# Bias products of the up rows dealt out among gate products, and another order of work in the tail

## What is computed

```python
x = x + s * g                      # first layer: a sparse gated product times a ternary gate
xn = _layernorm(x)
# s: a small recurrent net, width 64, depth 4
h = einsum('blv,dv->bld', xn, Win) + bin
for each of 4 layers:
    y = silu(layernorm(h, l1w, l1b))
    y = sconv(y, phazor, last_conv)            # a complex decaying scan along the sequence
    h = h + y * scl
    y = layernorm(h, l2w, l2b)
    y = silu(y @ W1.T + b1)                    # up, 64 to 256
    h = h + y @ W2.T + b2                      # down, 256 to 64
s = layernorm(h, lnl_w, lnl_b) @ Wout.T + bout # 64 to 512
g = silu(xn @ W.T + bias + low-rank experts)   # the gate, 512 to 512, the weights folded into one matrix
x = x + s * g
```

## Time and profile before

| | before |
|---|---|
| median of three executions | 606.12 us |
| lowest, highest | 604.01, 606.91 us |
| the profiled execution | 606.78 us |
| its span | 605.0 us |
| PE busy | 587.5 us (97%) |
| DVE busy | 486.8 us (80%) |
| ACT busy | 334.2 us (55%) |
| POOL busy | 170.8 us (28%) |
| mean granted clock | 0.989 |

### The profile page before, as it was taken

One profiled execution on the slowest core, in us unless ns is written; L12 is line 12 of the kernel. 1 busy time (PEld: TensorE's weight loads), 2 busy tenths in 40 slices (PEclk: granted clock), 3 DMA queues, 4 the chain that ended last, 5 costly groups with the idle time before them and its releaser, 6 DMA issues.

```text
span 605.0 us, 8900 instructions
## 1 busy us (share of the span) xinstructions
PE 587.5 (97%) x2868; PEld 455.7 (75%) x2868; DVE 486.8 (80%) x960; ACT 334.2 (55%) x567; POOL 170.8 (28%) x295
## 2 busy tenths in 40 slices
PE   7999999999999999999999999999999999999994
PEld 6887887888888888888888888887676555666542
DVE  6998899898788778788877878867889677887657
ACT  6879486266518626651852665285655344544430
POOL 2244002001000200100020010169954445454437
PEclk9999999999999999999999999999999799999998
DMA  8921000210030030003003000281220000000007
GB/s 341 333 69 45 2 0 1 71 35 2 1 104 0 0 104 0 0 0 104 0 0 104 0 0 0 72 304 54 54 55 1 0 1 1 1 1 1 1 1 277
DMA packets 18011, 32.37 MB, mean 53 GB/s; under 512 B 4054, under 2 KB 4566, under 8 KB 17980
## 3 DMA queue, kind: packets, MB, share of 16 engines
q1 hardware_dynamic: 17980, 32.00, 15.3%
HBM read 24.63 MB, written 7.36 MB: 53 GB/s over the span
## 4 chain that ended last, share of the span: by engine, by line
PE 73%; DVE 12%; POOL 4%; issue 4%; ACT 3%; DMA 2%; SPq 1%; DVEq 0%; POOLq 0%; ACTq 0%
PE ps_a L1859 15%; PE ps_b L1859 15%; PE ps_a L1892 15%; PE ps_b L2138 6%; PE ps_b L1899 3%; PE ps_a L2152 3%; DVE junk_d L1308 2%; PE ps_t L1878 2%; POOL arena L273 2%; PE ps_t L2146 2%; PE ps_a L2093 1%; PE ps_b L2100 1%; DMA arena<-in_f_w_t 1%; PE ps_a L2146 1%; ACT junk_a L977 1%
## 5 line engine op out<-in xcount | busy, mean ns | idle before, releaser
L1308 DVE TENSOR_SCALAR_CACHE_REDUCE junk_d<-k_buf,cand 128x1376 int8<-128x1376 f32 x56 | 91.9, 1640 | 0.3
L977 ACT ACTIVATE junk_a<-k_buf,cand 128x1376 int8<-128x1376 f32 x56 | 80.5, 1437 | 0.7
L956 ACT ACTIVATE s_buf<-ps_a 128x1376 f32<-128x1376 f32 x16 | 21.1, 1318 | 93.6 <-PE ps_a L1859 91.2
L1892 PE MATMUL ps_a<-wd_hi,zt_hi 128*128 128x512 f32 (+1 forms) x176 | 72.0, 409 | 0.1
L1892 PE MATMUL ps_a<-wd_hi,zt_lo 128*128 128x512 f32 (+1 forms) x176 | 69.2, 393 | 0.0
L1892 PE MATMUL ps_a<-wd_lo,zt_hi 128*128 128x512 f32 (+1 forms) x176 | 68.8, 391 | 0.0
L777 POOL TENSOR_TENSOR xres<-xres,gate 128x512 f32<-128x512 f32 x12 | 22.4, 1865 | 131.1 <-DVE gate L1434 131.1
L1859 PE MATMUL ps_a<-wg_hi,xt_hi 128*128 128x512 f32 (+1 forms) x192 | 51.9, 378 | 0.4 <-ACT s_buf L956 0.3
L1859 PE MATMUL ps_b<-wu_hi,xt_hi 128*128 128x512 f32 (+1 forms) x192 | 51.9, 378 | 0.0
L1859 PE MATMUL ps_a<-wg_lo,xt_hi 128*128 128x512 f32 (+1 forms) x192 | 50.8, 373 | 1.0 <-DVE wg_lo L1204 1.0
L1859 PE MATMUL ps_b<-wu_hi,xt_lo 128*128 128x512 f32 (+1 forms) x192 | 50.6, 372 | 0.0
(11 more groups left out here) (267 smaller groups left out, 1342.0 us busy)
## 6 DMA issues: line engine op xcount, KB each, us to landing
xres<-in_x SPq DMA_DIRECT2D x8, 512.0 KB, 3.4
out<-arena SPq DMA_DIRECT2D x16, 256.0 KB, 2.0
xin<-in_x SPq DMA_DIRECT2D x7, 512.0 KB, 4.0
x_scratch<-xres SPq DMA_DIRECT2D x6, 514.0 KB, 3.9
arena<-x_scratch SPq DMA_DIRECT2D x3, 1028.0 KB, 10.0
m_buf<-in_wg_t SPq DMA_DIRECT2D x2, 688.0 KB, 5.2
k_buf<-in_wg_t SPq DMA_DIRECT2D x2, 688.0 KB, 8.1
m_buf<-in_wu_t SPq DMA_DIRECT2D x2, 688.0 KB, 7.3
```

The costliest lines, as they stand in the source:

```text
L956: act.activation(s_buf[:, t, :], ps_a[:].rearrange("p a n -> p (a n)")[:, 0:INNER], ACT.Silu).then_inc(s_ready, 1)
L977: act.activation(junk_a[:], k_buf[:, 1, :], ACT.Sign, bias=c, scale=-1.0, accum_out=below[:, 1:2]).then_inc(act_step, 1)
L1308: dve.tensor_scalar(junk_d[:], k_buf[:, 0, :], c, -float(DROP), ALU.is_lt, ALU.add, accum_out=e).then_inc(cnt_dve, 1)
L1892: last = pe.matmul(ps_a[:, t, :], zs, ws[0:rows, c, :], start=(c == 0 and n == 0), stop=(c == CHUNKS - 1 and n == 2))
```

## The change

In phase 1 the eight bias products are no longer issued four at a time. Four go, each behind one gate product, ahead of `spread(q, c)`; one stands alone behind that spread; three go, each behind one gate product, behind `spread(n, d)`. Each product now counts `bc_ps`, and DVE waits for nine instead of three. `FILLS[1]` moves gate products: 7 to 5 ahead of the first spread, 1 and 1 between the spreads, 2 to 3 behind the second, 2 to 3 between up and down products.

In the tail the gate products behind the last down products go from two ahead of outputs 0 and 1 to one behind them. Behind the last spread two gate products and outputs 4 to 7 become outputs 4 and 5, three gate products, outputs 6 and 7. The last sum of tile 13 goes from DVE to POOL, that of tile 14 from POOL to DVE.

```diff
-FILLS = ((0, 0, 0, 0, 0, 0, 21), (2, 3, 7, 1, 2, 2, 0)) + ((2, 3, 7, 5, 5, 2, 0),) * 6 + ((2, 4, 3, 4, 2),)
+FILLS = ((0, 0, 0, 0, 0, 0, 21), (2, 3, 5, 1, 3, 3, 0)) + ((2, 3, 7, 5, 5, 2, 0),) * 6 + ((2, 4, 3, 4, 1),)
...
         def on_pool(m):
-            return m % 2 == 0 or m in (5, 7)
+            return m in (5, 7, 13) or m % 2 == 0 and m < TILES - 2
...
             def norm_biases():
-                dve.wait_ge(bc_ps, 3)
+                dve.wait_ge(bc_ps, 1 + 2 * DEPTH)
...
-            def norm_biases(layers):
-                pe.wait_ge(last_in, 16 * N_LAST)
-                for l in layers:
-                    for m in range(2):
-                        last = pe.matmul(bankx[0][:, 2 * l + m:2 * l + m + 1], w1[0:DIM, l, m * P:(m + 1) * P],
-                                         par.rearrange("p (l j) -> p l j", j=NPAR)[0:DIM, l, C_L2B:C_L2B + 1],
-                                         start=True, stop=True)
-                last.then_inc(bc_ps, 1)
+            def norm_bias(i):
+                if i == 0:
+                    pe.wait_ge(last_in, 16 * N_LAST)
+                l, m = i // 2, i % 2
+                pe.matmul(bankx[0][:, i:i + 1], w1[0:DIM, l, m * P:(m + 1) * P],
+                          par.rearrange("p (l j) -> p l j", j=NPAR)[0:DIM, l, C_L2B:C_L2B + 1],
+                          start=True, stop=True).then_inc(bc_ps, 1)
...
                 variances(n, d)
-                gates(fill[2])
+                if phase == 1:
+                    for i in range(4):
+                        gates(1)
+                        norm_bias(i)
+                gates(fill[2] - (4 if phase == 1 else 0))
                 spread(q, c)
                 if phase == 1:
-                    norm_biases(range(DEPTH // 2))
+                    norm_bias(4)
                 gates(fill[3])
                 spread(n, d)
                 if phase == 1:
-                    norm_biases(range(DEPTH // 2, DEPTH))
-                gates(fill[4])
+                    for i in range(5, 2 * DEPTH):
+                        gates(1)
+                        norm_bias(i)
+                gates(fill[4] - (3 if phase == 1 else 0))
...
                 down_unit(DEPTH - 1, 1, u)
-            gates(fill[4])
             pe.wait_ge(ln_o[0], DEPTH + 1)
             for m in range(2):
                 output_bias(m)
                 output(m)
+            gates(fill[4])
             variances(2 * DEPTH, 1)
...
             gates(5)
             spread(2 * DEPTH, 1)
-            gates(2)
-            for m in range(4, 8):
+            for m in range(4, 6):
+                output_bias(m)
+                output(m)
+            gates(3)
+            for m in range(6, 8):
                 output_bias(m)
                 output(m)
             gates(4)
```

## The result

The changed kernel takes 609.3 us in the median of ten executions (607.60 to 611.72), the kernel before 606.25 (603.73 to 606.99, ten as well). The ratio is 1.0059, 95% interval 1.0038 to 1.0079: 0.6% slower and clear of no change, where 605.4 was forecast, with 603.4 to 607.2 as its range. The profiled execution took 610.73 us (span 608.9) against 606.78 (span 605.0).

The account below looks back on a forecast made before the run. PE's clock fall in phase 1, the chain around it and DVE in the tail were taken to bound the kernel. 606.78 - 2.33 + 1.57 + 0.10 - 0.66 = 605.46, given as 605.4, range 603.4 to 607.2.

Parts of the forecast that it names:

- I take it that the clock stays. Term: -2.33.: Phase 1, up products to `fed`: streaming spread over the stretch keeps PE's clock up, saving the fall's 2.33 us.
- the sum's signs of being wrong: Phase 1: the forecast is wrong if the clock still falls, or the first spread is not later than 473.1.
- 1.57 for the alternation: Phase 1: four bias products at 0.505 each, less two gate products, start the first spread 1.57 us later.
- The three bare loads: Phase 1 bias products: three 128-column weight loads of about 0.107 make 0.32 a product, and the sum 604.7.
- 0.10 for the third gate product: Phase 1, behind the up products: the moved gate product costs 0.10 us, as down products would be ready 0.2 earlier.
- The last bias product would be written just before the sum that reads all eight: no further wait: Phase 1: last bias product written at about 478.8, the sum reading all eight now at 478.93, so no wait.
- The tail, "-0.66": Tail: earlier outputs and swapped sums end the last sum at 601.75 instead of 602.41; bounds -0.8 to +0.4 us.
- Product 4: Tail, DVE: outputs 4 and 5 directly follow the last spread, so product 4 comes at 589.33 instead of 590.17.
- product 8: Tail: one more gate product and output group start DVE's eight late products at 593.93 instead of 593.70.
- the waits for POOL: Tail: DVE waits 0.12 at the first sum and 0.55 at sum 14, instead of before's 1.04 + 0.43 lost.
- Rival 2: Phase 1: the clock falls all the same, -2.33 goes and +1.57 stays: 607.8 us, chance 0.12.
- The reading of before's run times: Before's runs, 604.01 to 606.91, fit a clock fall in some executions and not in others (604.45 without).

Follow-up runs that it names:

- kernel 2: The kernel before with only the changed kernel's tail order and swap of late sums, phase 1 as before: 603.32 us, ratio 0.9965.
- kernel 3: The kernel before plus four unread 512-column products between phase 1's second spread and the second four bias products: 603.98 us, ratio 0.9977.
- kernel 10: The whole changed kernel, but with bias products in groups of four and three instead of alternating with gate products: 604.92 us, ratio 0.9994 to before.
- kernel 4: Phase 1 edit on before's tail, plus one unread 512-column product behind each of the seven alternating bias products: 610.18 us, ratio 1.0075 to before.
- kernel 9: Phase 1 edit on before's tail, still alternating, each bias product on all 128 rows (bias twice the reference's): 606.04 us, ratio 1.0020 to before.
- kernel 7: The kernel before with only the last sums of tiles 13 and 14 swapped between DVE and POOL: 604.87 us, ratio 0.9985.
- kernel 1: The changed kernel's phase 1 edit alone, on the tail of before: 610.65 us, ratio 1.008 to before.
- kernel 5: Phase 1 edit on before's tail with seven of eight bias products left out (bias not the reference's): 606.09 us, ratio 1.0002 to before.
- kernel 11: The kernel before with bias products in the third up product's PSUM bank, PE waiting for DVE's sum ahead of that product: 604.60 us, ratio 0.9980.
- kernel 12: kernel 11 plus the changed kernel's tail and swap of sums: 602.87 us, ratio 0.9956 to before.
- kernel 6: Phase 1 edit on before's tail, with bias products in groups of four and three instead of alternating: 606.50 us, ratio 1.0018 to before.
- kernel 8: kernel 2 plus the four unread 512-column products of kernel 3: 603.78 us, ratio 0.9967 to before.

## Why the prediction was wrong

**The step that failed: "I take it that the clock stays. Term: -2.33."** The 2.33 itself is right (2.30 in kernel 2), and the reason given for the fall, thin work that counts as busy, fits kernel 3. But I asked only whether the stretch behind the first spread would stream more than before. By count it would, with four gate products for three. The stretch ahead of it streams less: from seven gate products in a row to one in 0.74 us, right behind narrow variance records. I had worked out that 0.74 as a cost and did not carry it over to what streams in that time. Instead of -2.33 the changed kernel's profile has the fall from 472.48 on, and it costs 2.77 - 1.57 = 1.2 up to `normed`, some 1.7 more up to the bias sum (of which the wait of 1.48 is the visible part) and 6.97 instead of 4.85 from the up products to `fed`, 2.1: 5.1 in all, 2.8 more than before's fall where the term had 2.3 less. Against the sum (605.46) the profiled execution is 5.27 late: 5.1 here and 1.06 for the fall at 578.29, less 0.43 that the tail gave beyond its term and 0.56 in the first layer, within 0.1. Of the sum's signs of being wrong, the clock that still falls is the one that came; kernel 10 shows the edit at fault, since without the alternation the same kernel is back at 604.92, and kernel 4 shows the clock to be the price, since the same instructions take 607 or 613.

**"1.57 for the alternation": right.** The round took 0.74, and kernel 4 has the 1.57 at full clock; kernel 9 settles the cause, the change between 64 and 128 rows, and its weight loads show that on 128 rows they run ahead of their product and on 64 they do not.

The Trainium skill (TensorE: Matmul & The Clock Gate, "Step-by-step: what each phase is for") has loads pulled ahead when the row groups do not conflict or when they go to the background weight buffer. The trace agrees that a load can be pulled ahead or not, but row groups that do not conflict cannot be the reason in kernel 9, where both products use all 128 rows; whether the second case is, no run shows. The three bare loads by the same page's section on LDWEIGHTS, 0.32 by the prediction's estimate, are too little: the price here is 0.505.

The smaller terms. **"0.10 for the third gate product"** was not measured by itself. **"The last bias product would be written just before the sum that reads all eight: no further wait"** had a margin of 0.1 us, which I called none; at half clock it became 1.48 us. A margin that small should have stood as a condition.

**The tail, "-0.66": right in its steps, 1.09 in the profile.** Product 4 0.91 earlier (0.84 forecast), product 8 0.18 later (0.23). What differs is the waits for POOL. From product 8 to the end of the last sum it is 7.44; twelve steps of 0.60 and 0.08 for the full length of the last are 7.28, so DVE waited 0.16 in all where the sum had 0.12 and 0.55. (The prediction's end, 601.75, is a slip besides: 593.93 + 7.20 + 0.67 is 601.80.) The swap by itself has 0.37 of the gain (kernel 7).

**The rivals.** Rival 2, the clock falls all the same, is what happened, with 0.12 for it and 607.8 as its time. It was priced too low because I let the fall keep its old length and let the added work run at full clock; the work that the edit adds lies inside the slow stretch and doubles. Its condition ("where its new slack lies the fall finds it") named the wrong place: there was hardly any slack, PE was busy for 13.28 of the 13.65 us. The reading of before's run times was right: 604.0 with the clock up, 606.3 as the median of the others. The missing conclusion was that an edit which makes the stretch thinner moves all executions into the second group.

What stays open: how thin a stretch has to be. The profiles show falls in two places, in phase 1 (before, after, kernels 1, 5, 7, 11 and 12) and in the last feeding (after, kernels 6, 7 and 8), and nobody varied the second. Kernels 5, 9, 10, 11 and 12 fall in half or more of their executions, while kernel 2, whose phase 1 is before's, fell in 4 of 12 where before on the same chip fell in 25 of 29. That is more than I would put down to the draw, and I have no cause for it that a run shows.

## What to carry to other kernels

Where the granted clock falls somewhere in the trace, cost an edit there twice: once in time and once in what it leaves streaming per microsecond, on both sides of the place, because work added inside a slow stretch costs double and the stretch grows. Keep small products on half of the rows together, or give them all the rows: each change of row group ahead of a wide product is paid on the chain. And look for the wait that makes a stretch thin: a result in another PSUM bank, which let the next products start, took 0.9 off phase 1 in the profiles (kernels 11 and 12 against 7) and, with the tail, gave the lowest median.

## What the runs showed of the hardware that was not expected

- TensorE's clock went from 2.4 to 1.2 GHz while PE was busy all the time (3.41 of 3.41 us ahead of the fall in after), behind records of one and two columns and single wide products between them. It had fallen before as well; the alternation made the fall 13.65 us long instead of 6.83.
- The same program falls in some executions and not in others: by their mean clock (0.996 or more), 22 of 98 executions of before had no fall that cost anything.
- Four products of 512 columns added to a wait made the kernel 1.9 us faster (603.98 against 605.86).
- A one-column fp32 product costs 0.505 us between wide products on 128 rows if it uses 64 rows (round 0.74, changed kernel), and 0.22 if it uses 128 (round 0.46, kernel 9). On 128 rows the first of its weight loads runs while the wide product ahead still streams (470.30, 0.24 ahead of its own product, kernel 9); on 64 rows the loads start with the product (470.75, changed kernel).
- A VectorE sum with both inputs in SBUF was held until GpSimd's running sum had ended: 1.65 us (before, GpSimd's from 595.51 to 596.61) and 1.60 us (kernel 7) instead of 0.68.
